# Sixteen-head attention: the score products in halves, issued in turn with halves of the second pass

## What is computed

```python
Q = query_input @ Wq + bq
K = key_value_input @ Wk + bk
V = key_value_input @ Wv + bv
Q = Q.reshape(b, sq, NH, HD).transpose(0, 2, 1, 3)
...
scores = jnp.einsum('bhqd,bhkd->bhqk', Q, K) / math.sqrt(HD)
mask = key_padding_mask[:, None, None, :]
scores = jnp.where(mask, -jnp.inf, scores)
attn = jax.nn.softmax(scores, axis=-1)
out = jnp.einsum('bhqk,bhkd->bhqd', attn, V)
out = out.transpose(0, 2, 1, 3).reshape(b, sq, H)
return out @ Wo + bo
```

## Time and profile before

| | us |
|---|---|
| median of 3 runs (1647.36 to 1651.45) | 1648.25 |
| device time of the profiled execution | 1658.71 |
| its span, first to last instruction | 1656.9 |
| TensorE busy in the span | 1521.7 |
| VectorE busy | 1144.9 |
| ScalarE busy | 802.8 |
| GpSimd busy | 583.2 |

### The profile page before, as it was taken

How to read it: one execution, slowest core, us unless ns; L and a number is a source line. 1 busy time by engine, 2 the same in 40 slices (tenths; PEclk the granted TensorE clock), 3 DMA queues, 4 the chain that set the end, 5 groups by cost and what they waited for, 6 DMA issues and landing times.

```text
span 1656.9 us, 34388 instructions
## 1 busy us (share of the span) xinstructions
PE 1521.7 (92%) x12742; PEld 1356.0 (82%) x12742; DVE 1144.9 (69%) x2350; ACT 802.8 (48%) x1527; POOL 583.2 (35%) x684
## 2 busy tenths in 40 slices
PE   3888898899999999788888699999989999999997
PEld 2777777799999999776777488888879999989997
DVE  3899987655655565137888458878866868676674
ACT  5777732244554455236666445445434444443442
POOL 3666650222211220047775212121114444443443
PEclk9999999899999999999999799999999999999999
DMA  6222253212323330152233411212135463544443
GB/s 189 64 79 80 73 183 121 77 55 74 100 92 101 101 102 26 51 197 77 85 94 96 144 61 53 78 53 71 35 73 109 88 130 83 116 101 96 101 94 68
DMA packets 118159, 152.11 MB, mean 92 GB/s; under 512 B 10090, under 2 KB 102852, under 8 KB 117508
## 3 DMA queue, kind: packets, MB, share of 16 engines
q1 hardware_dynamic: 110068, 127.48, 28.1%
q0 software_dynamic: 6560, 19.02, 4.0%
q10 hardware_dynamic: 1392, 3.70, 0.6%
HBM read 111.37 MB, written 38.80 MB: 91 GB/s over the span
## 4 chain that ended last, share of the span: by engine, by line
PE 39%; ACT 5%; DVE 5%; issue 5%; DMA 3%; SPq 1%; POOL 1%; DVEq 0%; ACTq 0%; POOLq 0%
PE psum L531 14%; PE psum L1811 4%; PE psum L1447 3%; PE psum L1795 3%; PE psum L498 3%; PE psum L506 3%; PE psum L1789 2%; PE psum L1772 2%; DMA arena_x<-wT_d 2%; ACT arena_y L1543 1%; DVE psum L2381 1%; ACT arena_y L1558 1%; PE psum L490 1%; PE psum L1492 1%; PE psum L1479 1%
## 5 line engine op out<-in xcount | busy, mean ns | idle before, releaser
L2152 POOL TENSOR_TENSOR d_g_parts<-arena_w,d_g_parts 128x512 fp32r<-128x512 f32 x128 | 167.1, 1305 | 253.5 <-ACT d_g_parts L2284 249.8
L531 PE MATMUL psum<-d_v_high,d_g_parts 128*128 128x256 f32 x1024 | 205.6, 284 | 3.3 <-DVE arena_x L1944 2.8
L531 PE MATMUL psum<-d_x_parts,d_v_high 128*128 128x256 f32 x1024 | 195.1, 288 | 6.7 <-issue 5.0
L531 PE MATMUL psum<-m_w_high,m_h_parts 128*128 128x256 f32 x1024 | 188.0, 284 | 0.0
L1213 ACT ACTIVATE arena_x<-psum,b_e 128x512 f32<-128x512 f32 x128 | 88.2, 689 | 190.2 <-PE psum L531 92.2
L531 PEld LDWEIGHTS psum<-d_v_high,d_g_parts 128*128 128x128 f32 x1024 | 168.5, 192 | 4.8 <-issue 3.0
L531 PEld LDWEIGHTS psum<-d_x_parts,d_v_high 128*128 128x128 f32 x1024 | 160.4, 193 | 13.7 <-issue 7.9
L1141 POOL DMA_INDIRECT arena_x<-x_d,slot_row x64 | 67.7, 1058 | 293.3 <-PE psum L1187 229.0
L531 PE MATMUL psum<-m_xF_parts,m_w_high 128*128 128x512 f32 x512 | 160.2, 394 | 2.1 <-DVE m_xF_parts L526 2.1
L531 PEld LDWEIGHTS psum<-m_w_high,m_h_parts 128*128 128x128 f32 x1024 | 160.7, 192 | 0.0
L531 PE MATMUL psum<-d_x_parts,d_vd_low 128*128 128x256 f32 x512 | 145.6, 284 | 0.0
(11 more groups left out here) (281 smaller groups left out, 3700.1 us busy)
## 6 DMA issues: line engine op xcount, KB each, us to landing
arena_x<-wT_d SPq DMA_DIRECT2D x128, 256.0 KB, 6.2
arena_y<-in_L_ffn_w SPq DMA_DIRECT2D x16, 1024.0 KB, 7.9
x_d<-arena_x SPq DMA_DIRECT2D x32, 256.0 KB, 2.2
y_d<-arena_x SPq DMA_DIRECT2D x16, 512.0 KB, 8.9
arena_x<-kv_d SPq DMA_DIRECT2D x16, 512.0 KB, 3.4
kv_d<-arena_x SPq DMA_DIRECT2D x9, 512.0 KB, 2.9
arena_x<-in_x SPq DMA_DIRECT2D x16, 256.0 KB, 2.9
arena_x<-in_ctx SPq DMA_DIRECT2D x16, 256.0 KB, 3.0
```

What stands on the lines that cost most here:

```text
L531: ins = nc.tensor.matmul(dst, left[a_], right[b_], start=start and k == 0, stop=stop and k == 2, skip_group_check=True)
L2152: nc.gpsimd.tensor_tensor(K["gP"][:, s % 4, 1], K["g"][:, s % 2], K["gP"][:, s % 4, 0].bitcast(F32), ALU.subtract).then_inc(d_gl, 1)
```

## The change

`scores` and `keys_first` become one function, `scores_and_less(sc, less)`, which issues half of the scores (`part` 0 on quarters 0 and 1, `part` 1 on 2 and 3) and, in turn with it, one half of a second pass on the other two quarters. A step calls it four times:

1. scores (u1, sequence 0, part 0) with the second pass (u2, sequence 0, half 1), which was in the step before;
2. scores (u1, 0, part 1) with (u2, 1, half 0);
3. scores (u1, 1, part 0) with (u2, 1, half 1);
4. scores (u1, 1, part 1) with (u1, 0, half 0).

I call each of them a joint call. `less_max` on VectorE is split in two parts of 1024 elements, one for each half of the scores; the transposed maxima move from bank 0 to bank 3. The query projection moves behind the first joint call, the input transpose of the unit that comes next (`un`, one step earlier than before) to the end of the step, the output projection between the third and the fourth joint call. ScalarE's and VectorE's programs follow that order: the residual comes behind the third reduction, and the query copies come early in the step. In step 0, the query copy of unit 0 now comes before the key copies on ScalarE. `X["q"]` gets four buffers and `X["aF"]` two. On GpSimd `rstd` is moved behind the copies for the next unit.

The new function, the new order on TensorE (`turn_input` is the old `to_feature` with its wait) and the reduction:

```diff
-        ARENA_X, ARENA_Y = 23040, 14464
+        ARENA_X, ARENA_Y = 23168, 14464
...
-        X["q"] = arena_x.take([P, 2, NC_, T])
+        X["q"] = arena_x.take([P, 4, NC_, T])
...
-        X["aF"] = arena_x.take([P, NC_, T])
+        X["aF"] = arena_x.take([P, 2, NC_, T])
...
+            def scores_and_less(sc, less):
+                if less:
+                    v, vb, half = less
+                    seq_done(pe, x_mT, v, vb)
+                    seq_done(pe, x_ex, v, vb, 2, 1) if half else seq_done(pe, x_ex, v, vb - 1, 2)
+                    less_quads = (2 * half, 2 * half + 1)
+                if sc:
+                    u, b, part = sc
+                    seq_done(pe, x_mx, u, b - 1, 2, part + 1)
+                    if part:
+                        seq_done(pe, x_mT, u, b - 1)
+                    for quad in (2 * part, 2 * part + 1):
+                        row = slice(32 * quad, 32 * quad + 1)
+                        nc.tensor.matmul(bank(quad), mask_one[row, :],
+                                         X["mask"][row, u.p, None, b * S:(b + 1) * S].broadcast_to([1, 4, S]),
+                                         start=True, stop=False, skip_group_check=True)
+                if less:
+                    for j in range(4):
+                        for quad in less_quads:
+                            rows = slice(32 * quad, 32 * quad + 32)
+                            nc.tensor.matmul(bank(4 + quad % 2)[:, j * S:(j + 1) * S], X["pick"][rows, j, :],
+                                             X["mT"][rows, vb, :], start=(j == 0), stop=False, skip_group_check=True)
                 for c in range(NC_):
+                    if sc:
+                        for quad in (2 * part, 2 * part + 1):
+                            rows = slice(32 * quad, 32 * quad + 32)
+                            got = nc.tensor.matmul(bank(quad)[:, c * 2 * S:(c + 1) * 2 * S],
+                                                   X["q"][rows, u.c % 4, c, b * S:(b + 1) * S],
+                                                   X["k"][rows, u.p, :, c * T + b * S:c * T + (b + 1) * S],
+                                                   start=False, stop=(c == 1), skip_group_check=True)
+                    if less:
+                        for par in range(2):
+                            j = 2 * c + par
+                            for quad in less_quads:
+                                rows = slice(32 * quad, 32 * quad + 32)
+                                ins = nc.tensor.matmul(bank(4 + quad % 2)[:, j * S:(j + 1) * S],
+                                                       X["k"][rows, v.p, par, c * T + vb * S:c * T + (vb + 1) * S],
+                                                       X["q"][rows, v.c % 4, c, vb * S:(vb + 1) * S],
+                                                       start=False, stop=(j == 3), skip_group_check=True)
+                if sc:
+                    got.then_inc(x_S, 1)
+                if less:
+                    ins.then_inc(x_less, 1)
...
-                seq_done(pe, x_mx, u, b)
-                nc.tensor.transpose(bank(0)[:, 0:P], X["mx"][:, b, :], ident).then_inc(x_mxT, 1)
+                seq_done(pe, x_mx, u, b, 2)
+                nc.tensor.transpose(bank(3)[:, 0:P], X["mx"][:, b, :], ident).then_inc(x_mxT, 1)
...
+                scores_and_less(u1 and (u1, 0, 0), u2 and (u2, 0, 1))
+                if u0:
+                    done(pe, x_xF, u0)
+                    project_features(bank(6), "L1_xattn_Wq", X["x4F"]).then_inc(x_q, 1)
+                elif u1:
+                    done(pe, x_r, u3.back(1))
+                    done(pe, x_qs, u1)
+                    d_turn(pe, D0, 6)
+                scores_and_less(u1 and (u1, 0, 1), u2 and (u2, 1, 0))
+                if u2 and not u1:
+                    seq_done(pe, x_mx, u2, 1, 2)
+                    d_similar(pe, D0)
+                if u2:
+                    done(pe, x_vs, u2)
+                    values(u2, 0)
+                if u1 and not u0:
+                    d_hash(pe, D0, 6)
+                if u1:
+                    turn_max(u1, 0)
+                else:
+                    if u2:
+                        seq_done(pe, x_mT, u2, 1)
+                        d_turn(pe, D1, 0)
+                scores_and_less(u1 and (u1, 1, 0), u2 and (u2, 1, 1))
+                if u2 and not u1:
+                    d_hash(pe, D1, 1)
                 if u3:
+                    if u0:
+                        done(pe, x_qs, u0)
                     else:
                         done(pe, d_hF, D0)
+                        done(pe, x_r, u3.back(1))
                     e_output(pe, u3)
+                scores_and_less(u1 and (u1, 1, 1), u1 and (u1, 0, 0))
                 if u2:
                     values(u2, 1)
                 if u2 and not u1:
                     d_weights_turn(pe, D0)
                     d_similar(pe, D1)
+                if un:
+                    done(pe, x_qs, u0)
+                    if u3:
+                        done(pe, x_r, u3)
+                    turn_input(un)
                 if u1:
                     turn_max(u1, 1)
...
-            def less_max(u, b):
-                seq_done(dve, x_S, u, b)
+            def less_max(u, b, part):
+                seq_done(dve, x_S, u, b, 2, part + 1)
                 seq_done(dve, x_mxT, u.back(1), b)
-                nc.vector.tensor_reduce(X["mx"][:, b, :].rearrange("p (q j) -> p q j", q=4)[:, :, 0:4],
-                                        psum[:, 0:4, :].rearrange("p q (k s) -> p q k s", s=S), AX, ALU.max,
+                quads_ = slice(2 * part, 2 * part + 2)
+                nc.vector.tensor_reduce(X["mx"][:, b, :].rearrange("p (q j) -> p q j", q=4)[:, quads_, 0:4],
+                                        psum[:, quads_, :].rearrange("p q (k s) -> p q k s", s=S), AX, ALU.max,
                                         negate=True).then_inc(x_mx, 1)
 
...
-                    less_max(u1, 0)
-                if u3:
-                    e_residual(dve, u3)
+                    less_max(u1, 0, 0)
+                    less_max(u1, 0, 1)
                 if u2 and not u1:
                     choose(dve, D0, 0)
                 if u2:
                     normalise(u2, 0)
                 if u1:
-                    less_max(u1, 1)
+                    less_max(u1, 1, 0)
                 if u2 and not u1:
                     choose(dve, D0, 1)
+                if u3:
+                    e_residual(dve, u3)
+                if u1:
+                    less_max(u1, 1, 1)
                 if u3:
                     e_result(dve, u3)
```

More of the change, by code:

```diff
@@ L1856, in step @@
-                if u1 and not u0:
-                    done(pe, x_r, u3)
-                    done(pe, x_qs, u1)
-                    d_turn(pe, D0, 6)
-                if u1:
-                    keys_first(u1, 0, 0)
+                scores_and_less(u1 and (u1, 1, 1), u1 and (u1, 0, 0))
                 if u2:
```

130 lines of the change are left out of this document (38 added, 92 removed).

## The result

| | before | changed |
|---|---|---|
| median, us | 1648.11 (10 runs, 1642.96 to 1651.45) | 1655.86 (10 runs, 1653.41 to 1663.47) |
| device time of the profiled execution | 1658.71 | 1653.63 |

The ratio is 1.0051, with a 95% interval of 1.0038 to 1.0064: half a per cent slower, where 0.9% faster was forecast. The two profiled executions stand the other way round; that of before lay 10 us above its median. I therefore set the changed kernel beside a second profile of before (x1_before_again, 1648.16 us, span 1646.4).

The account below looks back on a forecast made before the run. TensorE, without idle time at 16.83 us a step, was taken to bound stage E. Steps 3 to 15 gain 18.8, start -0.9, step 2 +1.0, end -3.5: 15.4 us less, 1632.9 us; range for 8 in 10 runs 1623 to 1643.

Parts of the forecast that it names:

- the joint call: Half of the scores beside half a second pass on TensorE: 1.53 us, or 2.61 with nothing overlapped.
- the free step: TensorE's step without splitting in stage E: 14.76 us against 16.83, a gain of 2.07 with nobody waiting.
- the half reduction: VectorE's reduction of 1024 elements: 1.22 us, or 1.14 counted from start to start.
- the place of the wait and its releaser: TensorE idle 1.15 us before the first `turn_max` in steps 5 to 8 and 13 to 16, ended by the half reduction.
- the wait of 1.26 in step 2: Step 2, without output projection: its fourth joint call waits 1.3 us for the third's exponential.
- the four rivals: Splitting hidden, 1624 us, chance 0.12; late answers every step, 1640, 0.20; little left, 0.09; program order, 1669, 0.07.
- little is left: Rival: joint calls cost 1.53 + 0.3 or the end loses twice as much, leaving within 5 us of before; chance 0.09.
- `e_result` 0.65 in the round of a split step: VectorE's `e_result` priced at 0.65 us within the 15.91 us round through TensorE and VectorE in steps with splitting.
- Start ... -0.9: Stage start: later key copies delay first scores some 1.8 us, smaller pieces give about half back; 0.9 us lost.
- +1.0: Step 2 takes 14.2 us against 15.20 despite its wait; 1.0 us gained.
- -3.5, between -2.5 and -5: Stage end: steps 16 and 17 up to `d_weights_turn`, delayed by waits and unit 14's late projection; 3.5 us lost.
- 27.2 up to the projection of unit 14: In step 17 unit 14's output projection follows `d_hash`, 27.2 us behind the mark at 1190.64.

Follow-up runs that it names:

- x13_pool: The changed kernel with GpSimd's output bias addition moved from the front of its step to behind the mask key's copy; 1649.27 us, ratio 1.0008.
- x3_fill: The changed kernel with four unused products ahead of the first `turn_max` in steps 5 to 8 and 13 to 15; 1650.72 us, ratio 1.0018.
- x11_warm_start: x2_spread's kernel with unused products of constants in step 1 alone (3 ahead of it, 4 ahead of its first `turn_max`); 1630.89 us, ratio 0.9885.
- x2_spread: The changed kernel with the sixteen splitting pieces spread over steps 3 to 16, one a step, two in 3 and 4; 1640.33 us, ratio 0.9958.
- x6_warm: x2_spread's kernel with unused products of constants where TensorE waits at both ends of the stage; 1633.61 us, ratio 0.9911.
- x12_warm_end: x2_spread's kernel with unused products of constants in step 17 alone (4, 5 and 8); 1635.05 us, ratio 0.9907.
- x8_best: x6_warm with unit 14's output projection replacing four products before step 17's second second-pass half, its residual before `choose`'s second part; 1630.56 us, ratio 0.9895.

## Why the prediction was wrong

**Right**: the joint call (1.54 for 1.53), the free step (14.73 for 14.76), the half reduction (1.23 for 1.22), the place of the wait and its releaser, the steps in which it stands, and the wait of 1.26 in step 2. None of the four rivals came true as it was written: the end did lose over twice as much, one of the conditions of "little is left", but a time within 5 us of before did not follow from it, nor would it have (15.4 less another 3.5 leaves 11.9). By the Trainium skill, "TensorE: Matmul & The Clock Gate", section "The mechanism", products start strictly in program order; the start at 1080.17 ahead of that at 1080.22 disagrees with it once more.

**Mis-sized: `e_result` 0.65 in the round of a split step.** It takes 1.24, because GpSimd's addition lies beside it. I had priced it from a row in which GpSimd was quiet. In before the addition follows `rstd` just as closely, but `e_result` comes only at 1069.14. GpSimd of the first profile of before:

```profile
1064.34 0.70 POOL L484 TENSOR_TENSOR X_st<-X_st,minus_half 128x2 f32<-128x2 f32 x1 [13.82 <-DVE X_st L464]
1065.00 1.41 POOL L1733 TENSOR_TENSOR arena_x<-arena_x,bo_b 128x256 f32<-128x256 f32 x2
```

In the new order one half reduction stands between the statistics and `e_result`, and I did not ask what GpSimd does then: the addition begins at 1055.05 and `e_result` at 1055.35. The Trainium skill has the rule, "SBUF — State Buffer", section "Who interferes with whom": an instruction such as `tensor_scalar` in VectorE's two-port mode and one of GpSimd exclude each other for their whole length. The trace agrees: 1.31 beside the addition, 0.73 without it (x13_pool), and each of the two instructions of `e_result` ends 0.14 to 0.15 behind the end of an addition beside it (1055.93 behind 1055.78, 1056.66 behind 1056.52). It cost 0.58 in each of seven steps, 4.1 us, of which my terms miss 0.54 a step.

**Left out: what a wait does to the clock.** I counted the wait in front of `turn_max` at its length. From one output projection to the next it took up to 2.6 us more (19.01 for 16.44, with one low stretch and half of another in it), and 4.9 us in steps 3 to 15 (x3_fill). That is 1.6 for each of the three waits with a low stretch behind them; the other four cost their length alone.

**"Start ... -0.9", with step 2 "+1.0".** Together 0.1 was to be gained, and 6.4 were lost. With the clock full behind the first stretch it is 33.6 (x11_warm_start), so 6 us of the loss are the clock's; whether the new order would gain at equal clock is not shown. What I missed is that projections and joint calls now stand where the clock is low, behind waits of 0.93, 1.49 and 1.33: the two query projections after the first take 3.71 and 3.33 for 1.92, the first joint call of step 2 takes 2.86 for 1.54. I saw the low clock (0.60), and took it as given instead of asking whether it would last.

**"-3.5, between -2.5 and -5" at the end.** It is -9.2 against before again, 5.7 more. With splitting spread the same stretch is 4.5 shorter. Of these, 1.3 is the wait in step 16 (15.85 for 14.55 between output projections). My text had step 16 last 15.9, but its 27.2 up to the projection of unit 14 has no room for the wait: x2_spread, without it, takes 27.7. The other 3.2 is low clock, and the spread kernel has 1.6 of it itself (x6_warm), which makes 4.8: values take 3.64 for 1.95, the output projection 3.05 for 1.99, `d_hash` 1.64 for 1.05, and smaller groups the rest. Without both, 33.1 of the 39.2 would be left, beside 33.5 forecast. That `choose` waits behind unit 14's residual and sets `d_weights_turn` was as forecast: TensorE waits 3.10 for it (L2386).

**Layer D**: 2.9 us longer in the profile, with the same code. Its length differs between executions of one kernel by more (430.4 and 436.7 in the two profiles of the changed one), so I take no cause from it. Whether the two idle times of TensorE there that no releaser explains (x12_warm_end) have a part in it stays open.

By size: 15.4 forecast; minus 3.8 for `e_result` in steps 3 to 15, 4.9 for the clock there, 6.5 at the start and 5.7 at the end gives -5.5, beside the -4.9 measured by marks. The range failed with it: apart from 1.0 us at the end all of it was built from terms at the full clock, and "little is left" had only 0.09. Waits made by the change itself should have had a rival of their own: that each can cost as much again in clock.

## What to carry to other kernels

When a change shortens TensorE's step, look for the engine whose round is now the longest and move its optional work (here two pieces of splitting a step) to one piece a step, before anything else: that alone made the difference between 0.5% slower and 0.4% faster. Count more than the length of a new wait on TensorE: behind some of them rows at granted clock 0.50 took up to twice as long (3.68 for 1.99). A few products without use in place of the wait can be worth it (5.1 us between the medians of x3_fill and the changed kernel), but take them out again when the wait goes: in x8_best they cost 2.8 us. And after a change of order look at GpSimd and VectorE side by side, for pairs that did not lie beside each other before.

## What the runs showed of the hardware

- A wait of only 1.79 us, in a stage in which TensorE is otherwise always busy, was followed by 3 us at granted clock 0.53; others of 1.64 were followed by none. Which of them it strikes differs between the two profiles of the changed kernel: near 1014, 1031 and 1158 us in the first, near 1013, 1047 and 1174 in the second. In both spread profiles neither the wait of 1.79 nor the one of 1.64 was followed by one. With waits of 1.20 and 1.06 (x13_pool) one such stretch was left in steps 3 to 15.
- `tensor_scalar` of 128x256 float32, both sides in memory on the chip: 0.73 us for two alone, 1.31 beside a GpSimd addition of 1.40 to 1.47. The half reduction (1.23 and 1.22 us) and the residual (0.69), which read from PSUM, took as long beside an addition as without one.
- Products on different quarters, issued in turn in mixed sizes, start at the pace of the quarters (0.21 to 0.22 us a round). In blocks of sixteen only the last 0.4 us overlap (2.19 for 1.53 and 1.08).
